# Down projection of a two-expert layer: one 512-column matmul for both halves of the weights, and the eviction split over ACT and DVE

## What is computed

```python
gate_logits = x @ gate_kernel                       # 8 experts
top_k_weights, top_k_indices = top_k(gate_logits, 2)
p = softmax(top_k_weights)
mult = silu(x @ w0[n]) * (x @ w1[n])                # 256 -> 512, per expert n
output = sum over the two chosen n of p_n * (mult @ wo[n])   # 512 -> 256
x = x + tanh(g_ffn) * output
```

## Time and profile before

| | us |
|---|---|
| median of 3 runs | 1425.06 |
| the three runs | 1422.74 to 1425.14 |
| time of the profiled execution | 1419.93 |
| its span, first to last instruction | 1418.3 |
| mean granted TensorE clock | 0.984 |

### The profile page before, as it was taken

One profiled execution on the slowest core, in us unless ns is written; L12 is line 12 of the kernel. 1 busy time (PEld: TensorE's weight loads), 2 busy tenths in 40 slices (PEclk: granted clock), 3 DMA queues, 4 the chain that ended last, 5 costly groups with the idle time before them and its releaser, 6 DMA issues.

```text
span 1418.3 us, 35550 instructions
## 1 busy us (share of the span) xinstructions
PE 1332.4 (94%) x9634; PEld 1168.6 (82%) x9635; DVE 808.1 (57%) x2522; ACT 695.4 (49%) x1778; POOL 890.7 (63%) x1389
## 2 busy tenths in 40 slices
PE   6999999999999999999829999999999999999996
PEld 5888888888888888888718888888888888888885
DVE  5688788888887887887733333333333333333332
ACT  3666666656666666666613333333333333333332
POOL 5588888888888888888853444444444444444443
PEclk9999999999999999999959999999999999999998
DMA  4133332233332333322677884333333333333332
GB/s 151 41 102 121 122 119 75 96 122 119 113 109 71 110 123 126 111 90 83 219 211 207 216 220 77 53 53 54 52 56 52 54 54 55 52 54 50 55 56 34
DMA packets 73956, 139.70 MB, mean 98 GB/s; under 512 B 11585, under 2 KB 55137, under 8 KB 71745
## 3 DMA queue, kind: packets, MB, share of 16 engines
q0 software_dynamic: 32064, 52.46, 19.0%
q1 hardware_dynamic: 39840, 86.05, 18.6%
q10 hardware_dynamic: 2016, 0.74, 0.2%
HBM read 68.95 MB, written 70.27 MB: 98 GB/s over the span
## 4 chain that ended last, share of the span: by engine, by line
PE 56%; issue 12%; DVE 11%; POOL 11%; ACT 4%; DMA 3%; DVEq 1%; POOLq 1%; SPq 0%; another core or an unknown queue 0%; ACTq 0%
PE banks L1322 25%; PE psB L1341 13%; PE banks L1156 4%; PE psT L1330 4%; POOL routed_rows L484 3%; PE psG L1307 2%; ACT prob L608 2%; PE banks L1108 2%; PE psT L1168 2%; ACT prob L612 2%; DMA out_dram<-ey,eid 2%; DVE qT L827 2%; POOL rs L426 1%; POOL rs L462 1%; POOL wrec L475 1%
## 5 line engine op out<-in xcount | busy, mean ns | idle before, releaser
L1322 PE MATMUL banks<-w_all,etT 128*128 x1620 | 433.2, 403 | 0.7 <-ACT etT L725 0.7
L1058 DVE TENSOR_TENSOR hgT<-psT,hgT 128x512 fp32r<-128x512 f32 x135 | 93.4, 692 | 425.0 <-ACT hgT L737 377.8
L1322 PEld LDWEIGHTS banks<-w_all,etT 128*128 128x128 f32 x1620 | 286.3, 189 | 51.3 <-issue 3.6
L537 POOL DMA_INDIRECT out_dram<-ey,eid x135 | 216.5, 1604 | 121.2 <-issue 46.1
L532 POOL DMA_DIRECT2D et<-routed_rows x135 | 79.2, 586 | 265.4 <-issue 202.3
L1341 PEld LDWEIGHTS psB<-w_all,hgT 128*128 128x128 f32 x1620 | 208.4, 188 | 18.4 <-issue 1.3
L1341 PE MATMUL psB<-w_all,hgT 128*128 x1620 | 217.9, 283 | 0.8 <-ACT hgT L737 0.8
L743 ACT ACTIVATE ey<-psB,ewt 128x256 f32<-128x256 f32 x135 | 64.0, 474 | 234.3 <-PE psB L1341 168.4
L731 ACT ACTIVATE hs<-banks 128x512 f32<-128x512 f32 x135 | 80.7, 597 | 185.5 <-PE psT L1330 183.6
L437 POOL TENSOR_TENSOR kbd<-kT,own 128x616 fp32r<-128x616 f32 x128 | 152.2, 1219 | 20.7 <-DVE kT L849 20.7
L1180 PE MATMUL psB<-vbd,probT 128*128 128x51 f32 x1280 | 158.1, 271 | 0.0
(11 more groups left out here) (163 smaller groups left out, 2307.1 us busy)
## 6 DMA issues: line engine op xcount, KB each, us to landing
split_weights<-w_part SPq DMA_DIRECT2D x16, 1536.0 KB
w_all<-split_weights SPq DMA_DIRECT2D x32, 768.0 KB
et<-routed_rows POOLq DMA_DIRECT2D x135, 129.0 KB
xb<-in_x_dram SPq DMA_DIRECT2D x32, 256.0 KB, 2.8
w_raw<-in_L_ffn_w_kernel_dram SPq DMA_DIRECT2D x32, 256.0 KB
out_dram<-x SPq DMA_DIRECT2D x64, 128.0 KB
w_raw<-in_L_ffn_wo_kernel_dram SPq DMA_DIRECT2D x16, 256.0 KB
cb<-in_ctx_dram SPq DMA_DIRECT2D x32, 77.0 KB
```

The costliest lines, as they stand in the source:

```text
L537: gp.indirect_dma_start(out=out, out_offset=bass.IndirectOffsetOnAxis(ap=eid[:, u:u + 1], axis=0), in_=ey[:, u % 2, :], in_offset=None, co ...
L1058: dve.tensor_tensor(hgT[:, 1].rearrange("p c q -> p (c q)"), psT[:], hgT[:, 0].rearrange("p c q -> p (c q)").bitcast(F32), ALU.subtract).t ...
L1322: m = pe.matmul(banks4[:, bank], etT[:, u % 2, a, c], weight(e, c, w, n), start=(j == 0), stop=(j == len(steps) - 1))
```

## The change

`down` computes the same sum in another grouping. The high part of the gated rows meets both parts of wo in one matmul of 512 columns: the moving operand is two runs of 256 columns, from the high and the low part of the weights (`weight_pair`), and the result fills all 512 columns of `psB`: rows-high x weights-high on the left, rows-high x weights-low on the right. The four matmuls of rows-low x weights-high (256 columns) add to the left half as before. So 4 matmuls of 512 and 4 of 256 columns stand in place of 12 of 256.

The two halves of `psB` must then be added and scaled. ACT scales the right half into `ey`, as large an operation as before, and increments the new semaphore `ey_low`. DVE then computes left half x `ewt` + `ey` (`y_sum`, one instruction over 128x256), behind `glu(t)` in its queue, and increments `ey_done`, which PE's next `down` and POOL's `add_rows` wait for.

```diff
--- before.py
+++ after.py
@@ -249,6 +249,7 @@
         passed = {e.engine: sem(f"passed{n}") for n, e in enumerate((nc.sync, nc.gpsimd, nc.vector))}
 
         tab, tab_done = sem("tab"), sem("tab_done")
+        ey_low = sem("ey_low")
         et_in, etT_ps, etT_hi, etT_lo, h0_ps, h1_ps = [sem("et_in0"), sem("et_in1")], sem("etT_ps"), sem("etT_hi"), sem("etT_lo"), sem("h0_ps"), sem("h1_ps")
         hs_done, hg_done, hgT_ps, hgT_hi, hgT_lo, ey_ps, ey_done, eid_done, added = (
             sem(n) for n in ("hs_done", "hg_done", "hgT_ps", "hgT_hi", "hgT_lo", "ey_ps", "ey_done", "eid_done", "added"))
@@ -740,7 +741,7 @@
                 act.wait_ge(ey_ps, t + 1)
                 if known(t, 2):
                     act.wait_ge(added, 16 * (t - 1))
-                act.activation(ey[:, u % 2], psB[:, 0:D], ACT.Copy, scale=ewt[:, u:u + 1]).then_inc(ey_done, 1)
+                act.activation(ey[:, u % 2], psB[:, D:2 * D], ACT.Copy, scale=ewt[:, u:u + 1]).then_inc(ey_low, 1)
 
             e_evac(0, 0)
 
@@ -1067,6 +1068,12 @@
                 dve.tensor_copy(eid[:, u:u + 1], et[:, u % 2, D:D + 1]).then_inc(eid_done, 1)
                 dve.tensor_copy(ewt[:, u:u + 1], et[:, u % 2, D + 1:D + 2]).then_inc(eid_done, 1)
 
+            def y_sum(t, u):
+
+                dve.wait_ge(ey_low, t + 1)
+                dve.scalar_tensor_tensor(out=ey[:, u % 2], in0=psB[:, 0:D], scalar=ewt[:, u:u + 1], in1=ey[:, u % 2],
+                                         op0=ALU.mult, op1=ALU.add).then_inc(ey_done, 1)
+
             e_low(0, 0)
 
             def tile(t, u, q):
@@ -1075,9 +1082,12 @@
                 if below(t, MOE_T - 1):
                     e_low(t + 1, (u + 1) % 4)
                 glu(t, u)
+                if known(t, 1):
+                    y_sum(t - 1, (u - 1) % 4)
 
             tiles(dve, tile)
             g_low(MOE_T - 1)
+            y_sum(MOE_T - 1, (MOE_T - 1) % 4)
 
 
         @block.tensor
@@ -1314,6 +1324,12 @@
                 at = ((c * 2 + part) * FR + run) * F + first
                 return w_of[:, bass.ds(e, 1), at:at + n].rearrange("p o f -> p (o f)")
 
+            wo_of = w_all[:].rearrange("p (e c) s r f -> p e c s r f", c=DC)
+
+            def weight_pair(e, c):
+
+                return wo_of[:, bass.ds(e, 1), c // 2, :, 2, c % 2 * D:(c % 2 + 1) * D].rearrange("p o s d -> p (o s) d")
+
             def up(t, u, e, n, bank, done):
                 steps = [(a, w, c) for a, w in PARTS for c in range(DC)]
                 for j, (a, w, c) in enumerate(steps):
@@ -1334,11 +1350,11 @@
                 pe.wait_ge(hgT_hi, t + 1)
                 if known(t, 1):
                     pe.wait_ge(ey_done, t)
-                steps = [(a, w, c) for a, w in PARTS for c in range(FC)]
-                for j, (a, w, c) in enumerate(steps):
-                    if (a, c) == (1, 0):
-                        pe.wait_ge(hgT_lo, t + 1)
-                    m = pe.matmul(psB[:, 0:D], hgT[:, a, c], weight(e, c // 2, w, 2, c % 2 * D, D), start=(j == 0), stop=(j == len(steps) - 1))
+                for c in range(FC):
+                    pe.matmul(psB[:, 0:2 * D], hgT[:, 0, c], weight_pair(e, c), start=(c == 0), stop=False, skip_group_check=True)
+                pe.wait_ge(hgT_lo, t + 1)
+                for c in range(FC):
+                    m = pe.matmul(psB[:, 0:D], hgT[:, 1, c], weight(e, c // 2, 0, 2, c % 2 * D, D), start=False, stop=(c == FC - 1), skip_group_check=True)
                 m.then_inc(ey_ps, 1)
 
             def expert_with_weights(t):
```

## The result

The changed kernel takes 1416.45 us (median of 5 runs, 1414.72 to 1418.14), the kernel before 1425.14 us beside it (5 runs, 1422.74 to 1426.27). The ratio is 0.9948, with a 95% interval from 0.9937 to 0.9959: 8.7 us or 0.6% faster by the medians. The prediction was 1419.0 us in a range from 1415.5 to 1423.5, with a gain of 6.1 us. The profiled execution took 1414.72 us, span 1413.1 us.

What follows compares the result with a forecast made beforehand. PE was taken to bound the expert stage, busy 400.00 of 400.00 us. Against the profiled execution 1419.93 - 6.6 + 0.5 = 1413.9 us; the same 6.1 us off the median 1425.06 gives 1419.0, range 1415.5 to 1423.5 with the first rival.

Steps and rivals of the forecast that it cites:

- Wide matmuls at 0.2317 us: PE's down projection: each of the four 512-column matmuls takes 0.2317 us, as in the up projection.
- The rival that a second run of the moving operand costs: PE's wide matmuls take 0.257 us each, so the kernel is 7.5 us slower, 1432.5 us; chance 0.06.
- Narrow matmuls at 0.1185 us behind them: PE's down projection: the last four 256-column matmuls run at 0.1185 us each, starting with the queue's lead.
- The late arrival of instructions as cause of the uneven pace: PE's down projection: instructions arriving too slowly cost 0.028 us a tile, which disappears with 512-column matmuls.
- only a fixed part: Rival on PE's down projection: only 0.021 us a tile is saved, 2.3 us in all, 1422.8 us; chance 0.14.
- One tile in eight has a longer piece; the change leaves that alone: Where PE's loop turns, a piece takes 1.62 instead of 1.39 us, and was expected to stay.
- 134 x 0.049 = 6.6 us: PE's gain: 0.049 us a tile (down projection 1.45 to 1.401 us) over the 134 on the path.
- DVE's step is free behind the gated rows: DVE's added instruction, 135 x 0.48 us, costs nothing in the steady tiles, with 1.9 us left before `g_low`.
- POOL: Scatters start at most 0.27 us later; their chain at 4.69 us keeps up with a 4.83 us tile; cost 0.
- The cover: After a late scatter, ACT's wait two tiles later still sees it landed, with 1.05 us of cover.
- The end, +0.52 us: Kernel end: `y_sum` stands between ACT's eviction of tile 133 and its scatter, adding 0.04 + 0.48 us.

Runs made afterwards that it cites:

- one_address_for_two: Kernel before with the second group of four matmuls reading the high weights again (4 address computations fewer a tile, 12 matmuls kept): 1420.92 us, ratio 0.9978.

## Why the prediction was right, and where it wasn't

**Wide matmuls at 0.2317 us: right.** Four take 0.91 to 0.93 us, 0.2275 to 0.2325 each. The rival that a second run of the moving operand costs is out: its threshold was 0.244.

**Narrow matmuls at 0.1185 us behind them: right.** Four take 0.47 us, 0.1175 each.

**The late arrival of instructions as cause of the uneven pace: right.** one_address_for_two removed it with the number of matmuls and of weight loads unchanged. The rival "only a fixed part" falls with that as the whole story. As a part of it, it was priced too low, and the late arrival too high: of the 0.054 us that the down projection lost on average, 1.445 - 1.426 = 0.019 came with the addresses, where I had 0.028, and 1.426 - 1.391 = 0.035 with the wide form, where I had 0.021. That the two errors nearly cancel is luck.

**"One tile in eight has a longer piece; the change leaves that alone": wrong.** This is the term that the sum lacked. The longer piece is 1.62 - 1.39 = 0.23 us, 15 times, 3.5 us. It goes away with the same four address computations as the uneven pace: PE's queue reaches the branch too late to have the next turn's instructions ready when the matmuls in hand run out. With half as many addresses to compute, and wide matmuls in hand, it has them. I had taken the lead of the queue as a matter within a tile and had not followed it to the turn.

**134 x 0.049 = 6.6 us: right in sum for what it covered.** 6.6 + 3.5 = 10.1 is what the mean tiles give, 134 x (4.906 - 4.831) = 10.1, and close to the 10.9 us that the stage lost in the two profiles.

**DVE's step is free behind the gated rows: right**, shown by leaving it out (0.1 us) and by moving it ahead (82 us).

**POOL: right for the steady tile, too easy on the bad case.** The scatters do keep up in the middle, in a tile of 4.82 us with 4.7 of their own. But I reckoned with one landing of 3.67 us behind a lag of 4.57. Single landings of 5 to 6.5 us occur, in the early part where the weights arrive and now and then later, and then a scatter chain with 0.14 us in hand needs, by estimate, (5.08 - 3.8) / 0.14 = 9 to (6.32 - 3.8) / 0.14 = 18 tiles to catch up. The cover was misread too: I looked at ACT's wait for the landing alone. DVE's wait for the same landing, before its copy into `eid`, comes about 1.0 us sooner in the tile (1104.27 against 1105.29 in the kernel before) and stands ahead of `glu`. The kernel before already spends 0.7 us in it between 740 and 830 us.

**The end, +0.52 us: right as a mechanism, small beside what decides there.** `y_sum` adds 0.52 us where scatters don't lag. In the profile of the changed kernel the end grew by 1.9 us, about 0.5 for `y_sum` and 1.4 for the lag behind the landing of 5.08 us, and leaving `y_sum` out gave a median 0.1 us away. How far the scatters lag at the end differs from run to run, with PE's old pace as with the new one; whether a faster PE makes it worse stays open.

**Net.** Forecast -6.6 + 0.5 = -6.1; measured in the tiles -10.1 (in the stage of the two profiles -10.9), at the end +0.5 and a lag of up to 1.4 more, and -7.8 to -9.3 in the medians. The gain came out 2.6 us larger than forecast, which by these figures is the 3.5 us of the turns less about 1 us more at the end.

## What to carry to other kernels

These are conclusions from this kernel. When a row of narrow matmuls steps unevenly while its weight loads are all short and early, count the address computations in front of it: the engine's own instruction queue can be the bound, and merging two matmuls over one stationary operand pays twice, in the row (0.054 us a tile here) and again at the next loop turn (0.23 us), where a lead is needed. A step added to another engine is free or expensive by its place in that queue: 65 us of DVE work cost nothing behind the product that PE waits for and 82 us ahead of it. Before speeding up the bound engine, look for the next chain with nearly its period: here scatters of 4.7 us under a tile of 4.82, so that, by estimate, a PE faster by more than 2 to 3% would gain nothing further. And follow every wait on that chain, not only the first one found: the one that reached PE stood in a third engine's queue, on a small copy.

## What the hardware showed beyond that

A scatter that adds to DRAM lands 3.8 us after its issue starts, the same scatter without the add 2.4 us, and its issue occupies POOL for 1.0 us instead of 1.6. In both forms single landings take much longer: the longest of a profile is 5.1 to 6.5 us with the add and 5.2 to 5.4 without it. And on DVE, `glu` behind `y_sum` without a wait between them starts before the recorded end of `y_sum`: 0.40 us after a start of 0.48 us length.
